# Row halves on TensorE, new bank homes, and products of ones in the waits of the lead

## The reference, cut to what matters

```python
h = gelu(cond @ W0 + b0); h = gelu(h @ W1 + b1)              # 32 x 128
att = softmax(h @ W2 + b2)                                   # 8 shares per sample
mixed = einsum('boi,bih->boh', einsum('bk,koi->boi', att, weight), x) + (att @ bias_k)[:, :, None]
# attention over the 32 tokens of each sample: 32 query heads, 8 key/value heads of 16,
# projections with sign(w) * mean|w| * scale; softmax(q k / 4) v; output projection likewise
y = bitnet_linear(attention(mixed), o_weight, o_scale)
x1 = x + y
c = grouped_conv1d(x1, 9 taps, 4 groups) + context(cond) + bias
# router: softmax over 8 experts, the two best; low-rank experts of rank 16
out = x1 + moe(c)
```

## Time and profile before

| what | value |
|---|---|
| median of 3 runs | 124.25 us |
| the runs | 123.92, 124.25, 126.06 us |
| the profiled execution | 124.09 us |
| its span (first to last instruction) | 122.3 us |
| TensorE busy | 109.3 us (89%) |
| VectorE busy | 98.0 us (80%) |
| ScalarE, GpSimd busy | 63.2 us, 48.7 us |
| chain that ended last | TensorE 56%, DMA 24%, VectorE 9%, issue 5%, ScalarE 3% |

### The profile page before, as it was taken

How to read it: one execution, slowest core, us unless ns; L and a number is a source line. 1 busy time by engine, 2 the same in 40 slices (tenths; PEclk the granted TensorE clock), 3 DMA queues, 4 the chain that set the end, 5 groups by cost and what they waited for, 6 DMA issues and landing times.

```text
span 122.3 us, 2847 instructions
## 1 busy us (share of the span) xinstructions
PE 109.3 (89%) x1008; PEld 83.4 (68%) x1008; DVE 98.0 (80%) x269; ACT 63.2 (52%) x147; POOL 48.7 (40%) x68
## 2 busy tenths in 40 slices
PE   1888999999997999995999999999999998699870
PEld 1765979999997977984887758776575535366510
DVE  0059999969949999979999899998967977379852
ACT  4547779894763878266473544656340302213400
POOL 1115920008206548938857999957600000000000
PEclk9999999999999999999999999999999999999998
DMA  3799999940000002000029869899599969982322
GB/s 81 226 336 411 427 383 411 402 150 3 5 0 1 0 5 86 0 3 5 0 86 180 171 145 201 220 191 189 177 201 191 238 213 201 243 184 88 121 109 113
DMA packets 18847, 19.56 MB, mean 160 GB/s; under 512 B 1488, under 2 KB 14480, under 8 KB 18448
## 3 DMA queue, kind: packets, MB, share of 16 engines
q1 hardware_dynamic: 17680, 17.27, 54.6%
q10 hardware_dynamic: 1152, 2.10, 5.2%
HBM read 15.17 MB, written 4.20 MB: 158 GB/s over the span
## 4 chain that ended last, share of the span: by engine, by line
PE 56%; DMA 24%; DVE 9%; issue 5%; ACT 3%; SPq 1%; DVEq 1%; ACTq 0%
PE bank L1404 10%; PE bank L1289 8%; DMA o_scale_row<-scale_all 7%; DMA x_turned<-x_all 7%; PE bank L1306 5%; PE bank L1360 5%; DMA rows_sb<-x_turned 4%; DMA o_scale_bc<-o_scale_row 4%; PE bank L1372 4%; PE bank L1455 3%; PE bank L1442 3%; PE bank L1420 3%; PE bank L1323 3%; PE bank L1324 3%; PE bank L1391 3%
## 5 line engine op out<-in xcount | busy, mean ns | idle before, releaser
L413 POOL TENSOR_TENSOR probs<-probs,row_inv 128x512 f32<-128x512 f32 x16 | 17.2, 1079 | 12.9 <-DVE row_inv L946 12.6
L1323 PE MATMUL bank<-mixed_hi,qkv_sign 128*128 128x256 f32 x72 | 17.6, 287 | 0.0
L1324 PE MATMUL bank<-mixed_lo,qkv_sign 128*128 128x256 f32 x72 | 16.9, 278 | 0.0
L395 POOL TENSOR_TENSOR keys_diag<-kv,keymask 128x512 f32<-128x512 f32 x8 | 8.4, 1052 | 14.5 <-DVE calm L911 13.7
L1404 PE MATMUL bank<-wo_sign,attn_hi 128*128 128x512 f32 x32 | 13.3, 416 | 0.8 <-DVE attn_lo L952 0.8
L1323 PEld LDWEIGHTS bank<-mixed_hi,qkv_sign 128*128 128x128 f32 x72 | 13.5, 188 | 0.6 <-issue 0.4
L1324 PEld LDWEIGHTS bank<-mixed_lo,qkv_sign 128*128 128x128 f32 x72 | 13.5, 188 | 0.0
L566 ACT ACTIVATE probsT<-bank 128x512 f32<-128x512 f32 x16 | 9.5, 596 | 7.2 <-PE bank L1372 7.2
L560 ACT ACTIVATE probs<-probs 128x512 f32<-128x512 f32 x16 | 10.1, 632 | 5.7 <-DVE probs L936 4.5
L1404 PE MATMUL bank<-wo_sign,attn_lo 128*128 128x512 f32 x32 | 12.6, 393 | 0.0
L930 DVE TENSOR_REDUCE row_max<-bank 128x16 f32<-128x512 f32 x16 | 10.6, 675 | 1.0 <-DVE safe_flag L885 0.7
(11 more groups left out here) (143 smaller groups left out, 234.8 us busy)
## 6 DMA issues: line engine op xcount, KB each, us to landing
rows_sb<-x_turned SPq DMA_DIRECT2D x18, 256.0 KB, 5.0
x_all<-in_x_rows SPq DMA_DIRECT2D x4, 512.0 KB, 9.1
x_turned<-x_all ACTq DMA_DIRECT2D x8, 256.0 KB, 3.1
out_rows<-x_all SPq DMA_DIRECT2D x8, 256.0 KB, 2.4
qkvT_sb<-in_qkvT SPq DMA_DIRECT2D x4, 384.0 KB, 6.3
rows_sb<-in_qkv_rows SPq DMA_DIRECT2D x1, 1536.0 KB, 10.3
qkv_sign<-x_turned SPq DMA_DIRECT2D x6, 256.0 KB, 6.5
rows_sb<-in_wo_rows SPq DMA_DIRECT2D x1, 1024.0 KB, 13.2
```

The lines of the kernel that those rows point to most:

```text
L413: pool.tensor_tensor(probs[:, t % 2, h, :, :], probs[:, t % 2, h, :, :], row_inv[:, t % 2, h, :].unsqueeze(2).to_broadcast([P, HALF, TOKENS]),
L1323: mm(dst, w, mixed_hi[:, ph, cols(i % 2, PAIR)], start=(ph == 0 and n % 2 == 0), stop=False)
L1324: last = mm(dst, w, mixed_lo[:, ph, cols(i % 2, PAIR)], start=False, stop=(ph == PHASES - 1 and n % 2 == 1))
```

## The change

- **Ones.** keep_busy multiplies the tile `ones` (filled by GpSimd's first memset) by itself. Its calls are now of 4 (before first_layer), 1 (before second_layer), 5 (between third_layer and spread_shares) and 3 (before mix(0, 0)).
- **Row halves.** For pairs 1 to 3 a product of mix is two: the weights are 64 rows of x, and the 64 columns of agg_diag that belong to these rows are streamed; the two halves go to banks 0 and 1, and full_mixed(i, b) takes the rows' half b of all phases, so it waits for both mix(i, 0) and mix(i, 1). turn_probs of tiles 3 to 6 and turn_conv of tiles 3 to 7 transpose 64-row halves into two banks.
- **Bank homes.** The eight banks are one tensor `halves`, in another order (PLACE), so that one instruction can read from two of them. attn_high and attn_low are one instruction of 512 elements each instead of two of 256. The convolution, the experts and the output take other banks.
- **Work that moves.** The low parts of pairs 2 and 3 go from VectorE to GpSimd (late_low_part); bound_o's arithmetic goes to GpSimd (bound_on_output), its sum over the row to ScalarE (sum_o_scales); residual(6) goes to GpSimd.
- **Order.** The lists of all engines are written in a new order.

```diff
-ODD_TURN = 3
+PLACE = (1, 0, 7, 4, 5, 6, 3, 2)
+
+HALVED = range(3, 7)
+CONV_HALVED = 3
...
+        halves = ctx.enter_context(nc.psum_tensor("halves", [P, 16, 2 * P], F32))
+        bank = [halves[:, 2 * n:2 * n + 2, :].rearrange("p a c -> p (a c)") for n in PLACE]
+
+        def two_halves(low, high):
+
+            return halves[:, low:high + 1:high - low, :]
...
+            to_window(6)
+            to_window(7)
             store(0)
-            to_window(6)
             store(1)
...
+            def late_low_part(i, b):
+                pool.wait_ge(hi_ready, 2 * i + b + 1)
+                pool.wait_ge(qkv_done, 3 * (i - 1))
+                pool.tensor_tensor(mixed_lo[:, 2 * b:2 * b + 2, cols(i % 2, PAIR)], mixed[:, 2 * b:2 * b + 2, :],
+                                   mixed_hi[:, 2 * b:2 * b + 2, cols(i % 2, PAIR)].bitcast(F32),
+                                   ALU.subtract).then_inc(late_lo_ready, 1)
+
+            def bound_on_output():
+                pool.wait_ge(bound_ready, 6)
+                pool.tensor_scalar(of_all, of_qkv, of_qkv, 4.0 * DIM, ALU.mult, ALU.mult).then_inc(bound_o_ready, 1)
+                pool.wait_ge(o_scales_summed, 1)
+                pool.tensor_scalar(of_y, of_qkv, by_o, float(HIDDEN), ALU.mult, ALU.mult).then_inc(bound_o_ready, 1)
...
+            def sum_o_scales():
+                act.wait_ge(o_scale_ready, 16)
+                nc.scalar.activation(junk_o[:, :], o_scale_bc[0:1, :], ACT.Abs, accum_out=by_o).then_inc(o_scales_summed, 1)
 
             def attn_high(t):
                 act.wait_ge(attn_done, 2 * (t + 1))
                 reached(act, y_done, t - 1)
-                for odd in range(2):
-                    nc.scalar.activation(part_of(attn_hi, t, odd), attn_of(t, odd), ACT.Copy).then_inc(attn_hi_ready, 1)
+                nc.scalar.activation(part_of(attn_hi, t), attn_of(t), ACT.Copy).then_inc(attn_hi_ready, 1)
...
+            copy_probsT(0, 1)
+            sum_o_scales()
+            scale_qkv(2, 2)
...
             def full_mixed(i, b):
-                dve.wait_ge(mixed_done, 2 * i + b + 1)
+                dve.wait_ge(mixed_done, 2 * i + (2 if i else b + 1))
                 dve.wait_ge(aggb_ready, min(i + 1, 3))
                 if i:
-                    dve.wait_ge(lo_ready, 2 * (i - 1) + b + 1)
-                bias = aggb_bc[:, cols(i, PAIR)].unsqueeze(1).to_broadcast([P, 2, PAIR])
-                v.tensor_tensor(mixed[:, 2 * b:2 * b + 2, :], ps_mixed[b][:, :].rearrange("p (a n) -> p a n", a=2), bias,
-                                ALU.add).then_inc(mixed_full, 1)
+                    low_reached(dve, 2 * i)
+                    bias = aggb_bc[:, cols(i, PAIR)].rearrange("p (a r n) -> p a r n", a=2, r=2)[:, :, b, :]
+                    v.tensor_tensor(mixed[:, :, :].rearrange("p f (a r n) -> p f a r n", a=2, r=2)[:, :, :, b, :],
+                                    ps_mixed[b][:, :].rearrange("p (f a n) -> p f a n", f=PHASES, a=2),
+                                    bias.unsqueeze(1).to_broadcast([P, PHASES, 2, P // 2]), ALU.add).then_inc(mixed_full, 1)
+                else:
...
             def bound_o():
-                dve.wait_ge(o_scale_ready, 16)
-                v.tensor_reduce(by_o, o_scale_bc[0:1, :], AX_X, ALU.add, apply_absolute_value=True).then_inc(bound_o_ready, 1)
...
-                v.tensor_scalar(safe_flag[:, 1:2], of_all, FINITE_BOUND, None, ALU.is_le).then_inc(bound_o_ready, 1)
-                dve.wait_ge(bound_o_ready, 6)
                 return dve.value_load(safe_flag[0:1, 1:2], min_val=0, max_val=1)
...
             def keep_busy(n):
                 for _ in range(n):
-                    mm(bank[7][:, 0:P], cond_sb[:, COND["W0"]], cond_sb[:, COND["W0"]], start=True, stop=True)
+                    mm(bank[7][:, 0:P], ones[:, :], ones[:, :], start=True, stop=True)
+
+            pe.wait_ge(ones_ready, 1)
...
-                    pe.wait_ge(mixed_full, 2 * (i - 1) + b + 1)
+                    pe.wait_ge(mixed_full, 2 * i)
+                    for a in tiles:
+                        for ph in (2 * b, 2 * b + 1):
+                            for r in range(2):
+                                rows = slice(P // 2 * r, P // 2 * (r + 1))
+                                at = (2 * ph + a) * P // 2
+                                last = mm(ps_mixed[r][:, at:at + P // 2], x_all[rows, 2 * i + a, ph * STEPS:(ph + 1) * STEPS],
+                                          agg_diag[rows, 2 * i + a, 2 * r:2 * r + 2, :].rearrange("p q o -> p (q o)"),
+                                          start=True, stop=True)
+                            if ph == 2 * b + 1 and a == 1:
+                                last.then_inc(mixed_done, 1)
+                    return
...
+                    for s in range(PER_TILE):
+                        last = nc.tensor.transpose(bank[6][:, s * P:(s + 1) * P],
+                                                   probs[:, t % 2, h, HEADS * s:HEADS * (s + 1), :], ident)
+                    last.then_inc(probsT_done, 2)
+                    return
+                if t == HALVED[0] and h == 0:
+                    pe.wait_ge(qkv_copied, BLOCKS * PAIRS)
                 for s in range(PER_TILE):
-                    last = nc.tensor.transpose(ps_probsT[:, s * P:(s + 1) * P],
-                                               probs[:, t % 2, h, HEADS * s:HEADS * (s + 1), :], ident)
-                last.then_inc(probsT_done, 1)
+                    for r in range(2):
+                        rows = slice(P // 2 * r, P // 2 * (r + 1))
+                        at = h * PAIR + s * P // 2
+                        last = nc.tensor.transpose(bank[3 if r else 6][:, at:at + P // 2],
+                                                   probs[rows, t % 2, h, HEADS * s:HEADS * (s + 1), :], ident[rows, rows])
+                        if s == PER_TILE - 1:
+                            last.then_inc(probsT_done, 1)
...
+                if t < CONV_HALVED:
+                    for s in range(PER_TILE):
+                        last = nc.tensor.transpose(ps_conv(t)[:, s * P:(s + 1) * P], conv_y[t % 2][:, s, :], ident)
+                    last.then_inc(convT_done, 2)
+                    return
+                if t == CONV_HALVED:
+                    pe.wait_ge(shifted, 2 * TILES)
+                elif t == LATE_TILES[0]:
+                    pe.wait_ge(probsT_copied, 2 * TILES)
+                else:
+                    pe.wait_ge(convT_copied, t - 1)
                 for s in range(PER_TILE):
-                    last = nc.tensor.transpose(ps_conv(t)[:, s * P:(s + 1) * P], conv_y[t % 2][:, s, :], ident)
-                last.then_inc(convT_done, 1)
+                    for r in range(2):
+                        rows = slice(P // 2 * r, P // 2 * (r + 1))
+                        last = nc.tensor.transpose(conv_homes(t)[r][:, s * P // 2:(s + 1) * P // 2], conv_y[t % 2][rows, s, :],
+                                                   ident[rows, rows])
+                        if s == PER_TILE - 1:
+                            last.then_inc(convT_done, 1)
 
...
+            keep_busy(4)
             first_layer()
+            keep_busy(1)
             second_layer()
             conv_context()
             third_layer()
+            keep_busy(5)
...
-            ffn_up(6)
-            turn_gated(5)
-            turn_conv(7)
+            ffn_up(7)
             ffn_down(5)
-            ffn_up(7)
```

495 lines of the change are left out of this document (257 added, 238 removed).

## The result

The changed kernel takes 133.72 us (median of four, 131.78 to 137.02); the kernel before, run beside it, 124.33. The ratio is 1.062 with a 95% interval of 1.057 to 1.067: 6% slower, where 120.3 us was predicted. The profiled execution took 131.96 us, its span is 130.2, against 124.09 and 122.3.

The account below looks back on a forecast made before the run. Bounds: the lead, then a chain through the output scales' store, load and VectorE's bound, then mainly TensorE, late also window loads and routing. 124.09 - 1.5 + 2.9 - 2.4 - 0.8 - 2.0 = 120.3 us, range 118.6 to 122.0.

Parts of the forecast that it names:

- The lead: Up to project(1, 0): added ones raise TensorE's clock before 9.7 us, project(1, 0) at 24.3 instead of 25.79; -1.5 us.
- rival 3: In the lead: ones are not enough, the clock rises at 16 us as before; 121.6 us, chance 0.10.
- The output scales: Before project_out(0): ScalarE waits for the broadcast row, TensorE idles 3.8 us, project_out(0) at 47.5; +2.9 us.
- Rival 2: At TensorE's pause before project_out(0): the clock falls to 1.2 GHz, costing 2.5 us; 122.8 us, chance 0.17.
- From project_out(0) to project_out(2)'s end: Stretch after the output scales: the new order's list is 19.1 us plus 0.3 of waiting; -2.4 us.
- To project_out(7): Stretch up to project_out(7): six halved turns save 0.8, merged attn_high and attn_low cover small waits; -0.8 us.
- The end: After project_out(7): window idle of 1.15 us goes, ffn_down(5) moves behind ffn_up(7), last tile 0.9 earlier; -2.0 us.
- The halves: Row halves in mixes and turns: a half mix takes 1.0 us, four turned blocks in halves 0.30 instead of 0.44.
- Rivals 1 and 4: Row halves: 1, fully side by side, 118.2 us, chance 0.20; 4, score's price throughout, 126.3 us, chance 0.10.
- Slower by over 2%: Whole kernel: the chance given to the change being slower by more than 2%; 0.08.

Follow-up runs that it names:

- e3: The changed kernel with 3 products of ones in the lead instead of 13; median 134.56 us.
- e1: The changed kernel with ScalarE's sum_o_scales moved from in front of scale_qkv(2, 2) to behind scale_qkv(2, 5); median 127.86 us.
- e2: The changed kernel with 20 products of ones filling TensorE's pause ahead of project_out(0); median 129.96 us.
- e9: e1 with GpSimd's spread_values(7) and residual(5) held until the first gate is done, and store_x1(5) three places later on ScalarE; median 127.11 us.
- e11: e1 with only spread_values(7) held on GpSimd until gate 0 is done, and turn_probs(7, 1) ahead of turn_gated(0); median 128.60 us.

## Why the prediction was wrong

Four of its five terms are wrong and one is missing. Their errors make up the miss in the profiled execution (span 130.2 against 118.5, 11.7 us): 1.5 for the lead, 1.6 for the output scales, 2.7 for the clock, 3.8 up to project_out(7) and 2.0 for the end.

- **The lead, -1.5: -0.3 measured, and a lottery.** The clock did rise early in the profiled execution, and the first high products started at 15.0 where I had 14.2. From there to project(1, 0) it took 10.4 us instead of 10.1. score(0) then ended at 30.7 (29.2 by my sum): 1.5 us. That ones cost nothing was wrong: with them the first mix starts 0.6 us later (e3, 9.56 against 10.15). And in six of the ten profiles with many ones the rise comes only at 19 to 23 us, which puts project(1, 0) 4.5 us later than in the other four. No term of mine had that: rival 3 came nearest, with a rise at 16 and 1.3 us.
- **The output scales, +2.9: +4.5 measured.** This is the step that failed first. The mechanism was right and stood in the prediction: the wait on ScalarE (5.60 us), what is queued behind it, TensorE idle (4.92, against 3.8), and +2.85 from the landing to project_out(0), as worked out (2.8). The row was there at +17.0 from score(0)'s end and not +15.5: VectorE had begun the stretch late, behind the guard, one of its tiny steps took 0.71 us, and the two DMAs 13.7 instead of 13.2. That is 1.6 us more than the sum had. The price was the place of one call: e1 has it behind scale_qkv(2, 5), where nobody waits.
- **The clock, 0 in the forecast: 2.7 us.** Rival 2 named it, its place, the level and 2.5 us; e2 shows 2.6. I gave it 0.17 and put it beside the forecast, while both hang on the same pause. With the idle of 3.8 us that the forecast itself had, the clock fell too (e3, 3.78 us of pause, 1.7 us of cost): the fall belonged into the sum. Nothing in the trace of before could tell that, since the longest pause behind its lead, 1.48 us, is followed by no fall.
- **From project_out(0) to project_out(2)'s end, 19.4: right.** Measured 22.1 in the changed kernel, less the 2.7 of the clock, is 19.4; e1, where it does not fall, has 19.4.
- **To project_out(7), -0.8: +3.0 measured.** This is the largest error. The term was added up from TensorE's groups only. The new order puts turn_gated(0) ahead of attend(7) and project_out(6), while the gate stands on VectorE between GpSimd's operations: pause 1.6 and fall 1.3 to 1.5. Before, the mask was as slow (1.20 us), but a turn and a project_out ran meanwhile. e9, with pause and fall gone, takes 43.8 us from project_out(0) to project_out(7), where my sum has 43.3.
- **The end, -2.0: 0 measured.** project_out(7)'s end to the last instruction is 27.7 us, as before (27.6). There is no idle time for a window in after, as predicted, but the chain of its tail is TensorE nearly throughout; where TensorE came to it sooner (e9, e11), tile 6's store and load took over and the stretch grew to 29 to 30 us.
- **The halves: right in size up to project_out(7).** 1.0 us a mix as taken, and 0.14 us gained for a turn of probabilities, as taken; the turns of the convolution gained nothing at the end. Rivals 1 and 4 are excluded.
- **The chances.** "Slower by over 2%" had 0.08. Rivals 2, 3 and 4 were each priced alone, against a forecast without them; that two losses could come together, and that a new order could open a pause elsewhere, had no share.
